# Half-wide block first, PE's expert program unrolled, and expert rows loaded two blocks ahead, in a cross-attention and mixture-of-experts kernel

## What is computed

```python
x = x + xattn(layernorm(x), ctx, ctx, mask, ...)
xf = layernorm(x).reshape(-1, 256)                    # 4096 tokens
ys = geglu(xf @ Ws1 + bs1) @ Ws2 + bs2                # shared expert, hidden 512
logits = (xf @ Wr + br) / 1.5
top_val, top_idx = top_k(logits, 2); top_w = softmax(top_val)
h = einsum('nd,edh->enh', xf, We1) + be1              # 12 experts, hidden 768
yE = einsum('enh,ehd->end', geglu(h), We2) + be2
x = x + ys + einsum('end,ne->nd', yE, w)              # w: top_w of the two picks, else 0
```

## Time and profile before

| what | us |
|---|---|
| median of 3 runs | 1150.32 (1148.36 to 1151.1) |
| the profiled execution's own time | 1145.5 |
| its span in the profile | 1143.6 |
| PE busy | 967.9 (85%) |
| DVE, ACT, POOL busy | 709.5, 568.7, 366.2 |

### The profile page before, as it was taken

How to read it: one execution, slowest core, us unless ns; L and a number is a source line. 1 busy time by engine, 2 the same in 40 slices (tenths; PEclk the granted TensorE clock), 3 DMA queues, 4 the chain that set the end, 5 groups by cost and what they waited for, 6 DMA issues and landing times.

```text
span 1143.6 us, 25763 instructions
## 1 busy us (share of the span) xinstructions
PE 967.9 (85%) x7515; PEld 704.6 (62%) x7516; DVE 709.5 (62%) x1834; ACT 568.7 (50%) x1276; POOL 366.2 (32%) x537
## 2 busy tenths in 40 slices
PE   5588888888898879788997989969996988988984
PEld 3233344444443437677777878858885877777874
DVE  5765768767787655555776746646463664655643
ACT  2126555555555664234535645645463664555643
POOL 5300120435426252073002333422333233332323
PEclk9769999999999999998999998989998999899998
DMA  5524326254442222167434424442342452433222
GB/s 149 140 71 105 75 50 155 79 123 122 125 100 74 67 90 92 40 243 272 148 111 130 123 41 121 118 128 38 49 129 41 114 130 40 121 79 83 48 41 38
DMA packets 105839, 115.57 MB, mean 101 GB/s; under 512 B 20092, under 2 KB 97864, under 8 KB 105552
## 3 DMA queue, kind: packets, MB, share of 16 engines
q1 hardware_dynamic: 85072, 66.08, 21.1%
q0 software_dynamic: 20064, 47.20, 16.6%
q10 hardware_dynamic: 560, 0.53, 0.1%
HBM read 73.64 MB, written 37.25 MB: 97 GB/s over the span
## 4 chain that ended last, share of the span: by engine, by line
PE 39%; issue 10%; DMA 4%; DVE 2%; SPq 1%; ACT 1%; POOL 1%; POOLq 0%; DVEq 0%; ACTq 0%
PE ff_psH L2193 25%; PE ff_psY L2204 13%; PE ff_psX L2178 2%; DMA ff_xrow<-expert_in 2%; DMA out_dram<-ff_ysc,ff_trow 1%; DMA ff_xrow<-xn 1%; DVE ff_actl L2387 1%; DVE ff_actf L2394 0%; POOL out_dram L2162 0%; SPq L1954 0%; ACT ff_ysc L2298 0%; DMA out_dram<-ff_x 0%; ACT ff_gel L2258 0%; PE ff_psB L2228 0%; DVE ff_ysb L2458 0%
## 5 line engine op out<-in xcount | busy, mean ns | idle before, releaser
L2193 PE MATMUL ff_psH<-xh,ff_wx 128*128 128x256 f16 (+1 forms) x1872 | 302.6, 273 | 62.2 <-issue 60.1
L2193 PE MATMUL ff_psH<-xl,ff_wx 128*128 128x256 f16 (+1 forms) x936 | 249.2, 273 | 0.0
L2193 PEld LDWEIGHTS ff_psH<-xh,ff_wx 128*128 128x128 f16 x1872 | 185.1, 103 | 88.5 <-issue 67.9
L1122 DVE TENSOR_REDUCE fast_negm<-fast_psS 128x2 f32<-128x512 f32 x256 | 169.7, 686 | 89.5 <-PE fast_psS L513 87.7
L2394 DVE SCALAR_TENSOR_TENSOR ff_actf<-ff_psH,ff_b1T,ff_gel 128x256 f32<-128x256 f32 (+1 forms) x234 | 106.2, 454 | 153.1 <-ACT ff_gel L2258 151.8
L884 ACT ACTIVATE fast_PT<-fast_psT 128x512 f32<-128x512 f32 x256 | 145.8, 598 | 75.5 <-PE fast_psT L545 75.2
L2162 POOL DMA_INDIRECT out_dram<-ff_ysc,ff_trow x78 | 124.9, 1601 | 181.9 <-ACT ff_ysc L2298 163.3
L2258 ACT ACTIVATE ff_gel<-ff_psH,ff_b1T 128x256 f32<-128x256 f32 (+1 forms) x234 | 105.8, 452 | 122.3 <-PE ff_psH L2193 109.2
L2204 PE MATMUL ff_psY<-ff_wx,ff_acth 128*128 128x256 f16 x840 | 140.5, 274 | 0.0
L513 PE MATMUL fast_psS<-fast_Kz,fast_Qs 128*128 128x512 f16 x256 | 101.1, 406 | 28.6 <-DVE fast_negm L1122 20.6
L2253 ACT ACTIVATE ff_acth<-ff_actf 128x256 f16<-128x256 f32 (+1 forms) x282 | 110.1, 390 | 22.6 <-DVE ff_actf L2394 21.2
(11 more groups left out here) (261 smaller groups left out, 1604.7 us busy)
## 6 DMA issues: line engine op xcount, KB each, us to landing
ff_st<-in_L_ffn_We_dram POOLq DMA_DIRECT2D x12, 1536.0 KB, 7.8
ff_xrow<-expert_in SPq DMA_DIRECT2D x40, 256.0 KB
ff_st<-in_L_ffn_We_dram POOLq DMA_DIRECT2D x12, 768.0 KB, 9.0
fast_Qs<-qstk SPq DMA_DIRECT2D x48, 128.0 KB
fast_xbuf<-in_x_dram SPq DMA_DIRECT2D x8, 512.0 KB, 5.0
fast_words<-in_mask_BxSxS_bk_dram SPq DMA_DIRECT2D x8, 512.0 KB, 3.9
fast_xres<-in_x_dram SPq DMA_DIRECT2D x8, 512.0 KB, 4.3
out_dram<-fast_x1s SPq DMA_DIRECT2D x8, 512.0 KB, 5.4
```

The source lines that it names most:

```text
L1122: nc.vector.tensor_reduce(negm[:, two(b), t, 2 * p:2 * p + 2], src, AX.X, ALU.max, negate=True).then_inc(sem["max_done"], 1)
L2193: mm = nc.tensor.matmul(psH[j % stage.banks][:, half * NB:half * NB + rows], a[:, dt, lo:lo + P], x[:, dt, 0:rows], start=(dt == 0 and i = ...
```

## The change

Four things are changed together. An expert's half block, if it has one, comes first and uses the upper half of the tiles, so the blocks of such an expert start 128 rows earlier in `xs`; each region gets 128 rows more at its front, which are zeroed by one more DMA. The loops are now a half body, one loop over blocks 0 to 2 (0 to 3 on SP and POOL) and rounds of three (four) blocks. PE's program is written out over the 12 experts, as ACT's and DVE's are. And SP issues the rows of block n + 2 and then the meta part of block n + 1 in block n. The core of the diff:

```diff
-REGION = N + NB
-X_ROWS = E * REGION + NB
-FEW = 4
 UN = P
+REGION = UN + N + NB
+X_ROWS = E * REGION + UN + NB
+FEW = 3
...
-            n = (units >> 1) if halves else (units + 1) >> 1
+            n, rest = (units >> 1, units & 1) if halves else ((units + 1) >> 1, 0)
+            few = FEW if halves else FEW + 1
...
+            if halves:
+                with eng.If(rest > 0):
+                    body(e, u, nc.s_assert_within(at, 0, NBLK - 1, skip_runtime_bounds_check_because=
+                                                  "an expert with rows has a first block"), None, UN)
             lead = 0
...
-            if lead < FEW // 2:
-                with eng.Fori(lead, FEW // 2) as t:
-                    own(t)
-            with eng.If(n > FEW // 2):
-                with eng.Fori(FEW // 2, FEW) as t:
-                    own(t)
-                with eng.If(n > FEW):
-                    with eng.Fori(1, N // NB // FEW) as group:
-                        with eng.If(n > group * FEW):
-                            with eng.Fori(0, FEW) as t:
-                                own(group * FEW + t)
-            if halves:
-                with eng.If((units & 1) > 0):
-                    body(e, u, block_at(n), None, UN)
+            with eng.Fori(lead, few) as t:
+                own(t)
+            with eng.If(n > few):
+                with eng.Fori(1, -(-N // NB // few)) as group:
+                    with eng.If(n > group * few):
+                        with eng.Fori(0, few) as t:
+                            own(group * few + t)
...
-        sp.dma_start(xs[E * REGION:, :].rearrange("(j p) d -> p j d", p=P), zeros[:]).then_inc(zeroed, 16)
+        sp.dma_start(xs[E * REGION + UN:, :].rearrange("(j p) d -> p j d", p=P), zeros[:]).then_inc(zeroed, 16)
+        sp.dma_start(xs[0:E * REGION, :].rearrange("(e r) d -> r e d", r=REGION)[0:UN],
+                     zeros[:, 0:1, :].to_broadcast([P, E, DX])).then_inc(zeroed, 16)
...
         def load_rows(n):
             until(expert, "xT_mm", of(expert, "xT_mm", n))
-            rows = xs[bass.ds(table(sp, start_i, n, X_ROWS - NB), NB), :].rearrange("(j p) d -> p j d", p=P)
-            sp.dma_start(xrow[expert][:], rows[:, :, 0:D]).then_inc(expert.sem["x_loaded"], 16)
+            sp.dma_start(xrow[expert][:], rows_at(n)[:, :, 0:D]).then_inc(expert.sem["x_loaded"], 16)
+
+        def load_meta(n):
             until(expert, "w_link", of(expert, "w_link", n))
             until(expert, "w_set", of(expert, "w_set", n))
             until(expert, "t_set", of(expert, "t_set", n))
...
+        def load_next(e, u, n, beside, rows):
+            load_rows(n + 2)
+            load_meta(n + 1)
+
         load_rows(0)
+        load_meta(0)
         store_out(NSH - 2)
         load_x1(NSH - 1)
+        load_rows(1)
         store_out(NSH - 1)
-        experts(sp, None, lambda e, u, n, beside, rows: load_rows(n + 1), halves=False)
+        experts(sp, None, load_next, halves=False)
...
-                            mm = nc.tensor.matmul(psH[j % stage.banks][:, half * NB:half * NB + rows], a[:, dt, lo:lo + P],
-                                                  x[:, dt, 0:rows], start=(dt == 0 and i == 0), stop=(dt == DT - 1 and i == 2))
+                            mm = nc.tensor.matmul(psH[j % stage.banks][:, (half + 1) * NB - rows:(half + 1) * NB], a[:, dt, lo:lo + P],
+                                                  x[:, dt, NB - rows:], start=(dt == 0 and i == 0), stop=(dt == DT - 1 and i == 2))
...
-        experts(pe, weights_ready, lambda e, u, n, beside, rows: ffn(expert, n, w1[u], w2[u], (expert, n + 1), rows))
+        experts(pe, weights_ready, lambda e, u, n, beside, rows: ffn(expert, n, w1[u], w2[u], (expert, n + 1), rows),
+                unrolled=True)
```

More of the change, by code:

```diff
@@ L1875, in feed_forward @@
     units = sb("units", [P, E], FP32)
+    half_i = sb("half_i", [P, E], I32)
+    half = sb("half", [P, E + 1], FP32)
+    change = sb("change", [P, E], FP32)
+    ahead = sb("ahead", [P, 1], FP32)
     place_i = sb("place_i", [P, E], I32)
@@ L2200, in ffn @@
                 stage.until(pe, "actl", of(stage, "actl", m, j + 1))
-                for i in range(rows // P):
+                for i in range((NB - rows) // P, NBT):
                     terms = [(acth, wb[0]), (acth, wb[1]), (actl, wb[0])]
@@ L2252, in high @@
                     stage.until(act, "y_mm", of(stage, "y_mm", m))
-                nc.scalar.activation(acth[:, j, 0:rows], actf[:, j % 2, 0:rows], ACT.Copy).then_inc(stage.sem["acth"], 1)
+                nc.scalar.activation(acth[:, j, NB - rows:], actf[:, j % 2, NB - rows:], ACT.Copy).then_inc(stage.sem["acth"], 1)
             for j in range(n):
@@ L2257, in ffn @@
                 stage.until(act, "h_mm", of(stage, "h_mm", m, j + 1))
-                nc.scalar.activation(gel[:, j % 2, 0:rows], psH[j % stage.banks][:, NB:NB + rows], ACT.Gelu,
+                nc.scalar.activation(gel[:, j % 2, NB - rows:], psH[j % stage.banks][:, 2 * NB - rows:2 * NB], ACT.Gelu,
                                      bias=gate_bias[:, j:j + 1]).then_inc(stage.sem["gelu"], 1)
@@ L2325, in tables @@
             nc.vector.tensor_copy(units[:], units_i[:])
+            nc.vector.memset(half[:, E:E + 1], 0.0)
+            then(nc.vector.tensor_scalar(half_i[:], units_i[:], 1, None, ALU.bitwise_and))
+            then(nc.vector.tensor_copy(half[:, 0:E], half_i[:]))
+            nc.vector.tensor_scalar(ahead[:], half[:, 0:1], float(-UN), float(UN), ALU.mult, ALU.add)
+            nc.vector.tensor_tensor(change[:], half[:, 1:E + 1], half[:, 0:E], ALU.subtract)
             dve.wait_ge(cleared, 1)
@@ L2393, in ffn @@
                 stage.until(dve, "gelu", of(stage, "gelu", m, j + 1))
-                nc.vector.scalar_tensor_tensor(actf[:, j % 2, 0:rows], psH[j % stage.banks][:, 0:rows], bias[:, j:j + 1],
-                                               gel[:, j % 2, 0:rows], ALU.add, ALU.mult).then_inc(stage.sem["act"], 1)
+                nc.vector.scalar_tensor_tensor(actf[:, j % 2, NB - rows:], psH[j % stage.banks][:, NB - rows:NB], bias[:, j:j + 1],
+                                               gel[:, j % 2, NB - rows:], ALU.add, ALU.mult).then_inc(stage.sem["act"], 1)
                 if j:
```

37 lines of the change are left out of this document (21 added, 16 removed).

## The result

The changed kernel took 1136.72 us (median of 5 runs, 1132.11 to 1137.69), the kernel before 1148.36 (5 runs beside it, 1143.79 to 1151.1): a ratio of 0.9897, with a 95% interval of 0.986 to 0.9934. It became faster by about 12 us, where 40 were forecast; the time lies inside the range of 1091 to 1138, at its slow end. The profiled execution took 1134.73 us.

The account below looks back on a forecast made before the run. PE was taken to bound the experts' stage (522.4 us): 432.0 work + 26.8 gaps + 8.6 clock + 1 rows + 10.2 GpSimd's chain + 0.5 waits = 479.1. Saving 43.3, less 3 at the start, gave 1110 us, range 1091 to 1138.

Parts of the forecast that it names:

- What is late next: GpSimd's chain around half blocks makes the meta transfer late for VectorE; 1.7 us at six places, 10.2 us.
- psY: PE's second matmul phase of a block, time over 4.09 us (full) or 2.13 (half), VectorE late; 10.2 us forecast.
- psH: PE's first matmul phase of a block, time over 8.02 us (full) or 4.19 (half); 9.1 us forecast.
- gaps: PE's idle time ahead of a block's first matmul in the experts' stage; forecast to fall to 26.8 us.
- GpSimd's release: GpSimd frees the half block's rows 13.2 us after the full block's end, 9.3 + 2.9 + 1.0.
- feels a part: PE, with three PSUM banks of lead, feels part of VectorE's 2.9 us lateness; 1.7 a place, bounds 0 and 3.5.
- Rows two ahead: SyncE issues rows once their buffer is free; PE's 5.3 us of waiting for rows goes, 1 is left.
- Start: Ahead of the experts' stage: extra zeroing delays expert 0's rows, 2 us, and new table operations cost 1; together +3.
- C: Rival: PE's jump over the group body misses at each expert entry; about 11 us slower, 1161; chance 0.07.
- E: Rival: only the rows ahead matter and PE's jumps merely change place; 1148, no change; chance 0.04.
- D: Rival: GpSimd's chain is hidden, the start covered, the clock costs 4; about 1092, below 1098; chance 0.13.
- B: Rival: losses return in part by GpSimd's chain at 3.5 a place, overtaken fetches or low clock; 1120 to 1140; chance 0.22.

Follow-up runs that it names:

- late_load: The changed kernel with GpSimd issuing the next expert's weight load after the expert's first block, not at the expert's start; 1110.66 us, ratio 0.9653.
- late_busy: late_load with four small unneeded fills on GpSimd at each expert's start, each waited for; 1164.28 us on another chip, ratio 0.98.
- mid_load: The changed kernel with the weight load issued inside the expert's first block, right after GpSimd releases the meta buffer; 1130.49 us, ratio 0.9836.
- meta_two: The changed kernel with two meta buffers, the weight load left in place; 1147.02 us on another chip, ratio 0.9681.
- ahead_only: The kernel before with rows issued two blocks ahead, nothing else; 1184.56 us on another chip, ratio 0.9993.
- unrolled_only: The kernel before with PE's expert program written out, nothing else; 1128.43 us, ratio 0.9799.
- late_meta_two: The changed kernel with two meta buffers and the weight load after the expert's first block; 1141.23 us on another chip, ratio 0.9613.

## Why the prediction was right in direction and wrong in size

**The failed step** is the term "What is late next", mis-sized at 10.2 us (1.7 x 6): it measured 37.0, 6.2 a place. The mechanism was as forecast: full block, half block, full block, and the meta transfer late behind GpSimd's start of an expert. The count of six was right in part by luck: experts 2, 4, 6, 7 and 9 stalled as forecast, expert 11 did not, and expert 0 did, whose half block follows a shared block. Five of the six stalls lie above the upper bound of 3.5 a place, so the bound failed with the value. Against the forecast stage of 479.1, the terms moved by +26.8 (psY), +6.7 (psH), -5.3 (gaps), -1.0 (rows) and +1.1 (rest): 28.3 us, of which this one is nearly all.

Three parts of the working failed, to be seen in expert 4, counted from the full block's end at 755.93:

- GpSimd's release: 13.2 forecast, 16.2 measured (771.95 + 0.19). The cost of an expert's start had been counted from its first shown instruction (`taken`, 734.43 to 737.29 in the earlier trace rows). The loop's end, the tests and the table load ahead of it are no busy time, so no row has them; `taken` comes at 11.8, 2.5 later than GpSimd's next block would (9.3). From `taken` to `filled` it is 3.2, against 2.9 forecast.
- The meta transfer: 2.4 us to landing forecast, 5.20 measured; with the 0.2 us more until its issue, the values are there at 22.3 in place of 16.3. The 2.4 was the landing of 264 KB of zeros, and it is a fair price for the meta transfer where no load is near (1.7 to 3.5 us in late_load). Here the transfer starts 3 to 4 us behind the issues of a 2.3 MB load. That the two meet could have been read off the order of GpSimd's steps.
- PE's share: "feels a part" was wrong. VectorE wanted the values at 15.3 (forecast 13.4) and got them 7.0 late; PE stalled for 7.5. PE's second phase needs `actl` of all pairs, and those of the last three come behind the late step (by 782.20).

Each of the first two alone keeps a good part of the stall, and they do not add up: of the 27.3 us of psY that late_load took away, GpSimd's time brings back 13.4 (late_busy) and the bytes 20.6 (mid_load). That is why half a cure (mid_load) did nothing for the stage, and both together gave 24 us (late_load).

**Gaps: right in sum.** 26.8 forecast, 21.5 measured. They are to be held against 54.6 before, not 60.1: the row of 60.1 in the earlier trace rows also holds 6.4 us within the first phases of three half blocks, which the prediction read as lying ahead of blocks. That leaves 20.5 us of low clock before (26.9 - 6.4), where the prediction had 23. Into expert 1, 6.0 and 6.5. The three skipped half bodies, 3.6 each: 3.64 in expert 3, 3.67 in expert 10, but 0.07 in expert 8. Expert 5 has no half block either, which the prediction left out; its jump took 332 ns, that of expert 8 220 ns. The jump in expert 8 is 0.07 us of gap here and 3.1 to 3.4 in late_busy, mid_load and meta_two, with the same program on PE. What makes it cheap or dear was not tried. Expert 4's end, 3.8 and 3.72. Entries into half blocks, 4.2 forecast, 1.2 in sum ahead of them (some more within, below); half body into loop, 2.0 and 2.8. By the figure of a store of 2048 instructions, which the prediction quoted from the Trainium skill (Runtime: NRT & Kernel Launch, "Instruction fetch mechanics"), no jump over the half body would cost anything; the two branches of 2667 and 2714 ns do not agree with it.

**psH: too low.** 8.6 of low clock and 0.5 of small waits were forecast, 15.8 measured. About 9 are low clock, as forecast in sum: the half block of expert 1 behind the 6.5 us gap took 6.76 us for 4.19, four full blocks 0.4 to 2.6 longer, two of them behind a stall in psY and not behind a gap. The other 6.7 are short waits at a full granted clock, 0.2 to 1.2 each in the other seven half blocks and 1.0 in expert 8's first block. In experts 2, 8 and 9 the wait is mostly "issue", 0.7 to 1.0 us within the block; that is a cost of the entry, and the forecast had it ahead of the block. In experts 4, 6, 7 and 11 it is for VectorE's `actf`, 0.6 to 0.7 us, which no term held. The gaps' price on the clock was uneven. Stretches of the changed kernel, in the columns of the earlier trace rows:

```profile
731.29:739.32 8.03, 8.03 (x74) 7.24 (x75) 5.47 (x14) 5.64 (x14) 3.15 (x4) 1.00 0.30 38
...
836.78:847.34 10.56, 10.56 (x74) 8.52 (x75) 5.47 (x14) 5.64 (x14) 3.90 (x5) 0.75 0.33 38
```

The first follows a gap of 3.64 us and runs at the full clock, the second one of 3.72 us at 0.75 of it; the gap of 3.67 us in expert 10 was followed by 0.75 too. The granted clock over the stage stayed at 0.94, where 0.97 was forecast; it reached 0.98 in late_load, where the stalls were gone.

**Rows two ahead: right** in that the 5.3 us went and the meta transfer behind them was not delayed, yet incomplete: alone the edit is worth nothing (ahead_only), since the gaps take its gain, and with the rest it is worth 15.8. The sum had it as 4.3. No run took the two-ahead issue out of the changed kernel itself, so these are prices in its neighbours.

**Start: 3.9 us for 3 forecast, and not told from the scatter.** unrolled_only does the work of the kernel before ahead of the stage and starts it at 611.85, 3.1 us later than before; mid_load does that of the changed kernel and starts it at 609.64, 3.0 us earlier than it. So the agreement is luck. SyncE issues the extra zeros at 598.47 and expert 0's rows at 606.75, 8.3 us later, against 3.6 before, and PE waits 0.6 us for these rows. PE is 1.0 us later already at the first shared block (489.27 against 488.29) and 4.4 us later at the sixth (545.46 against 541.02); but unrolled_only is as late at both (489.3 and 545.1) without any of the change's work there.

**The rivals.** C (slower) fell: the branches at the end of the loop took 0.33 us in the median and 0.81 at most, as its argument against had it. E fell too: "issue" went down by 45.4 us (60.1 - 14.7), and no jump took it over. D asked for a hidden GpSimd chain; late_meta_two comes near that (4.2 us of psY left), and its ratio gives 1106 on the first chip, not 1092. B is what came, 1120 to 1140, but its first loss alone, at 6.2 us a place where it had 3.5.

The total of late_load, 1110.66 us, is near the forecast of 1110. That is the forecast with its 10.2 in the one term that failed (9.7 measured), while the errors of the others cancel; it says nothing for the prediction of the change itself.

## What to carry to other kernels

When the gaps of the bounding engine close, the helper engines' chain between two blocks becomes the next limit, and it is tightest where the shortest block stands: count that chain from the end of the last block's transfer through loop ends, table loads and every DMA issue, not from the first busy row. A small transfer on which work waits is priced beside the large one that is issued just ahead of it, not by its landing where nothing else is under way. And a second buffer for a few bytes (stage -24 us), or the large load moved behind the first block (-24 us), did more than the whole change (-15 us). So did one line of the change by itself: PE's program written out took 17.5 us off the stage of the kernel before. Parts of a change that are tried one by one show such a loss at once.

## What was not expected of the hardware

- A transfer of 8 KB took 5.20 us to land behind a load of 2.3 MB issued 3 to 4 us before it, and 7.74 us where the load was issued around it (mid_load), against 1.7 to 3.5 us for the same transfer in late_load where no load was issued just ahead.
- One and the same jump of PE, over expert 8's half body, left a gap of 0.07 us in the changed kernel, 3.4 in mid_load and meta_two and 3.1 in late_busy, all with the same program on PE. Why stays open.
- Two gaps of PE of nearly the same length, 3.64 and 3.72 us, were followed by granted clocks of 1.00 and 0.75 over the next 72 matmuls. What tells them apart stays open.
- The same kernel, on one core, took 1150.28 us on one chip and 1186.47 and 1186.95 on two others, in medians. The experts' stage did not differ (changed kernel 507.4 and 507.1, late load 483.3 and 484.3); it began at 609 to 614 us on the first chip and at 646 to 655 on the others. In ahead_only (646.4) against before (608.7), 14.9 of the 37.6 us are there at the first shared block, and the rest comes between the second and the third (513.1 to 548.9 against 498.2 to 506.6), where ScalarE waits for something that the profile does not name, up to 20.1 us at a time. Why was not looked into.
